# Adapter + mixture-of-experts + quantized FFN on one core: collecting in three segments of four, two and two blocks, five routing groups, three tile output buffers, and a new hand-off order

## The reference, cut to what matters

```python
h  = x @ W.T + (x @ A[adapter].T) @ Bm[adapter].T * scale          # layer 1, condition
s  = sigmoid(h @ gate_w.T); top_scores, sel = top_k(s, 2)          # routing, 2 of 8 experts
for k in range(2):
    xs = h * top_scores[:, k]
    routed += w2[sel] @ (silu(w1[sel] @ xs) * (w3[sel] @ xs))
x1 = x + routed + ws2 @ (silu(ws1 @ h) * (ws3 @ h))
y  = einsum('bct,bcd->bdt', x1, w[cond])                           # layer 2, condition
u  = relu(quant(fwht(y)) @ ternary(w_up).T) ** 2
x2 = x1 + quant(fwht(u)) @ ternary(w_down).T
```

## Time and profile before

| what | value |
|---|---|
| median of 3 runs | 372.76 us (369.45 to 373.54) |
| the profiled execution | 371.4 us |
| its span in the trace | 369.3 us |
| outside of the span | 2.1 us |
| mean granted TensorE clock | 0.97 of full speed |

### The profile page before, as it was taken

How to read it: one execution, slowest core, us unless ns; L and a number is a source line. 1 busy time by engine, 2 the same in 40 slices (tenths; PEclk the granted TensorE clock), 3 DMA queues, 4 the chain that set the end, 5 groups by cost and what they waited for, 6 DMA issues and landing times. The chain is left out here.

```text
span 369.3 us, 8740 instructions
## 1 busy us (share of the span) xinstructions
PE 318.8 (86%) x2564; PEld 296.8 (80%) x2564; DVE 278.4 (75%) x735; ACT 217.7 (59%) x528; POOL 204.0 (55%) x211
## 2 busy tenths in 40 slices
PE   7899999995757999949998989799987798887974
PEld 7798999894657999938997979799976687776863
DVE  0957999999587998743654557678956999997995
ACT  4574343232215467606566658788866888956964
POOL 1100059899899898930000667888818888883000
PEclk9999999999689999987999999999999999998999
DMA  7980692522237859547398885997757556664013
GB/s 187 359 330 1 228 313 84 198 74 76 88 104 209 261 192 303 191 114 215 109 286 265 190 171 89 197 211 141 173 145 137 70 75 107 123 101 79 30 58 114
DMA packets 53803, 59.02 MB, mean 160 GB/s; under 512 B 9856, under 2 KB 47744, under 8 KB 53760
## 3 DMA queue, kind: packets, MB, share of 16 engines
q1 hardware_dynamic: 40752, 40.81, 36.1%
q0 software_dynamic: 12432, 17.57, 23.4%
q10 hardware_dynamic: 576, 0.10, 0.2%
HBM read 32.87 MB, written 25.59 MB: 158 GB/s over the span
## 5 line engine op out<-in xcount | busy, mean ns | idle before, releaser
L1378 POOL DMA_INDIRECT X<-ys,POSY x64 | 101.9, 1592 | 74.7 <-DMA ys<-YS 43.0
L1026 POOL DMA_INDIRECT hs<-ZF,POS x64 | 64.3, 1005 | 10.6 <-issue 10.1
L1025 POOL MEMSET PACE<- 128x512 f32 x64 | 34.8, 543 | 33.7 <-DVE POS L1014 33.7
L1278 PE MATMUL UP<-WH,XSH 128*128 x142 | 42.9, 302 | 0.4 <-issue 0.2
L1278 PE MATMUL UP<-WH,XSL 128*128 x142 | 39.9, 281 | 0.0
L1278 PE MATMUL UP<-WL,XSH 128*128 x142 | 39.8, 280 | 0.0
L792 PE MATMUL AUX<-WH,ZR 128*128 128x264 f32 x128 | 26.0, 297 | 10.3 <-ACT ZF L815 10.1
L1258 ACT ACTIVATE XSH<-TR 128x512 fp32r<-128x512 f32 (+1 forms) x36 | 21.4, 594 | 22.2 <-PE TR L1245 20.0
L815 ACT ACTIVATE ZF<-AUX 128x264 f32<-128x264 f32 x32 | 12.0, 387 | 36.6 <-PE AUX L802 16.4
L1263 DVE TENSOR_TENSOR XSL<-TR,XSH 128x512 fp32r<-128x512 f32 (+1 forms) x36 | 24.4, 678 | 10.3 <-ACT XSH L1258 7.3
L792 PEld LDWEIGHTS AUX<-WH,ZR 128*128 128x128 f32 x128 | 21.3, 198 | 11.9 <-issue 11.2
(11 more groups left out here) (262 smaller groups left out, 997.0 us busy)
## 6 DMA issues: line engine op xcount, KB each, us to landing
ys<-YS SPq DMA_DIRECT2D x42, 256.0 KB
XIN<-hs SPq DMA_DIRECT2D x71, 132.0 KB
X<-in_x SPq DMA_DIRECT2D x8, 512.0 KB, 8.0
out<-X SPq DMA_DIRECT2D x16, 256.0 KB, 2.2
X<-in_WE SPq DMA_DIRECT2D x8, 384.0 KB, 7.9
ZF<-in_xT SPq DMA_DIRECT2D x4, 512.0 KB
XR<-in_xT SPq DMA_DIRECT2D x4, 512.0 KB
hs<-ZERO SPq DMA_DIRECT2D x8, 132.0 KB
```

What stands on the lines that cost most here:

```text
L1025: e.memset(PACE[:, :], 0.0).then_inc(S["pac"], 1)
L1026: e.indirect_dma_start(hs, bass.IndirectOffsetOnAxis(ap=POS[:, k, t0 + t:t0 + t + 1], axis=0), HT[:, slot + t, :], None).then_inc(s_st[b % ...
L1278: mm = e.matmul(UP[s % 2][:, c * 256:c * 256 + 256], v[:, r % 2, k, c * P:(c + 1) * P], w[:, cols], start=(n == 0), stop=(n == 5))
L1378: e.indirect_dma_start(X1[:, tt, :], None, ys[p], bass.IndirectOffsetOnAxis(ap=POSY[:, k, tt:tt + 1], axis=0), compute_op=ALU.add).then_in ...
```

## The change

- `SEGMENTS` (4, 8) becomes (4, 6, 8): blocks 0 to 3, 4 and 5, 6 and 7 are collected from three ys tensors. `CARRIED` follows: 7, 15, 23. The second segment waits for pairs 0 to 27, the third for all 36. Pairs 13 to 19 are stored three times and pairs 20 to 27 twice. `count`, `jumps` and `home` run three times.
- `GROUP_SIZES` (2, 2, 2, 2) becomes (1, 1, 2, 2, 2): five routing chains.
- YS gets a third buffer (`NY = 3`), and `y_out` waits for the store of three pairs before.
- `TIME` is new throughout, so the order on each engine is new; the places that matter are shown below.

```diff
-GROUP_SIZES = (2, 2, 2, 2)
-SEGMENTS = (4, 8)
+GROUP_SIZES = (1, 1, 2, 2, 2)
+SEGMENTS = (4, 6, 8)
...
+PIECES = max(2, PARTS)
+BIGGEST = max(_b - _a for _a, _b in zip((0,) + SEGMENTS, SEGMENTS))
...
-    "home": [103.4764, 149.4409],
+    "home": [105.6110, 129.0289, 158.4598],
...
+NY = 3
...
-              for i, n in enumerate((TILES[0] + 2 * CARRIED[0], TILES[1]))]
+              for i, n in enumerate([TILES[0] + 2 * CARRIED[0]] + [2 * c for c in CARRIED[1:-1]] + [TILES[1]])]
...
-        YS = sb("YS", [P, 2, 2, D])
+        YS = sb("YS", [P, NY, 2, D])
...
-                pieces = ((ORIGIN, LINE[:, PARTS, 0:NE], 0), (START[:, 0, :], LINE[:, 0, 0:NE], P * TILES[0]),
-                          (START[:, 1, :], LINE[:, 1, 0:NE], 0))
-                if p:
-                    pieces = ((START[:, 0, :], LINE[:, 0, 0:NE], 0), pieces[2])
-                else:
-                    pieces = pieces[0:2]
+                pieces = [(START[:, c, :], LINE[:, c, 0:NE], P * TILES[0] if p == 0 else 0) for c in range(p + 1)]
+                if p == 0:
+                    pieces = [(ORIGIN, LINE[:, PARTS, 0:NE], 0)] + pieces
...
-            return [(1, 2 * i)] + ([(0, TILES[0] + 2 * i)] if i < CARRIED[0] else [])
+            return [(k, (0 if k else TILES[0]) + 2 * i) for k in reversed(range(PARTS)) if i < CARRIED[k]]
...
-            put = 16 * sum(len(homes(q)) for q in range(r % 2, r - 1, 2))
+            put = 16 * sum(len(homes(q)) for q in range(r % NY, r, NY))
...
-                if r >= 2:
-                    e.wait_ge(s_y[r % 2], put)
+                if r >= NY:
+                    e.wait_ge(s_y[r % NY], put)
```

More of the change, by code:

```diff
@@ L57 @@
 TIME = {
-    "home": [103.4764, 149.4409],
[L59 to L85, removed]
+    "home": [105.6110, 129.0289, 158.4598],
+    "last_tables": [150.8858],
+    "jumps": [100.6280, 111.3651, 144.8223],
+    "count": [79.3267, 98.0063, 136.3136],
@@ new lines @@
+    "make_mask": [8.7495],
+    "load_later": [15.9370],
+    "make_origin": [15.1470],
+    "weight_sums": [44.7497],
+    "weight_total": [47.9447],
+    "ternary": [50.3145],
+    "clear_bd": [112.1478],
+    "load_x": [2.3500, 3.2900, 13.3920, 20.9885, 39.3378, 39.8078, 105.4953, 154.5733],
+    "x_hi": [8.5090, 9.5650, 23.5675, 34.8153, 48.1582, 65.2068, 78.9802, 90.7745],
+    "x_lo": [9.6185, 10.7610, 24.8810, 36.6353, 57.1475, 67.6288, 82.8875, 92.2764],
+    "xa": [11.2710, 14.0190, 29.7990, 40.9592, 58.4400, 69.3503, 84.1800, 94.5724],
@@ L104 @@
+        116.7551, 137.4616, 142.0748, 169.6800, 172.4670],
     "s_out": [
[L105 to L113 removed]
@@ L114 @@
-    "fold_hi": [23.6227],
-    "fold_lo": [23.9137],
+        24.2775, 37.8862, 49.1080, 67.0253, 77.0912, 81.9485, 84.4739, 88.6438, 96.4583, 103.6855, 116.0016,
+        120.0114, 140.6218, 143.2733, 170.5995, 173.6655],
+    "load_xT": [2.8200, 14.9970, 15.4670, 40.2778, 40.7478, 58.4400, 68.9213],
+    "fold_turn": [7.0760],
+    "fold_copy": [7.7350],
+    "fold": [12.6750],
+    "fold_shared": [8.6790],
+    "shared_hi": [12.8970],
+    "shared_lo": [15.2270],
+    "fold_hi": [14.2390],
+    "fold_lo": [14.9800],
@@ L462, in adapter_moe_quant_ffn @@
         s_st = [sem(f"p_st{i}") for i in range(RING)]
-        s_y = [sem(f"p_y{i}") for i in range(2)]
+        s_y = [sem(f"p_y{i}") for i in range(NY)]
         s_g = [[sem(f"p_g{k}{i}") for i in range(4)] for k in range(2)]
@@ L1349, in y_put @@
                 for k, slot in homes(r):
-                    e.dma_start(ys[k][slot * P:slot * P + n, :].rearrange("(c q) d -> q c d", q=P), YS[:, r % 2, 0:tiles, :])\
-                     .then_inc(s_y[r % 2], 16)
+                    e.dma_start(ys[k][slot * P:slot * P + n, :].rearrange("(c q) d -> q c d", q=P), YS[:, r % NY, 0:tiles, :])\
+                     .then_inc(s_y[r % NY], 16)
             at("sync", "y_put", r + 2, y_put)
         def puts_done(e, pairs):
-            for j in range(2):
-                e.wait_ge(s_y[j], 16 * sum(len(homes(q)) for q in range(j, pairs, 2)))
+            for j in range(NY):
+                e.wait_ge(s_y[j], 16 * sum(len(homes(q)) for q in range(j, pairs, NY)))
         def plan_collect(p):
```

122 lines of the change are left out of this document (64 added, 58 removed), and 248 rows, old and new, of the table TIME.

## The result

The changed kernel takes 377.17 us (median, 374.32 to 378.48) against 372.73 for the kernel before on the same chip: ratio 1.011 (95% interval 1.007 to 1.016), slower by a little over 1%. The forecast was 365 with a range up to 374. The profiled execution took 378.48 us (span 376.7) at a mean granted clock of 0.958; that of before took 371.4 (span 369.3) at 0.97. The one is the slowest of its four runs and the other lies under its median, so the spans differ by 7.4 us and the medians by 4.4. The spans of one kernel differ from run to run (the kernel before: mostly 367 to 373 us), so a difference of one to three us between two traces can be chance.

What follows compares the result with a forecast made beforehand. It took GpSimd's scatters, then its collects, as two chains in a row, VectorE close behind. Span 369.3 - 7 = 362.3, with 2.1 outside it 364.4, plus half of 1.4 for the profiled execution: 365, range 353 to 374.

Steps and rivals of the forecast that it cites:

- The first scatter: Start of GpSimd's scatters: needs block 0 alone, so it comes at 40.5 us in place of 49.8.
- The scatters: GpSimd starts 9 us earlier, then starves by as much for VectorE's positions; last scatter at about 161, term +1 (-6 to +6).
- From the last scatter to the first collect: Pairs 13 to 19 with added stores on SyncE's queue: +1 us (-2 to +5), first collect at 205.
- the slower case: Rival: VectorE and the queue make scatters and first stores late; last positions 141.7, loads up to 5 us later; 376, chance 0.12.
- VectorE's added steps at 0: Third home (4.9 us) and last_tables' four more instructions (0.9) lie beside the scatters' end: cost 0, at most 5.8.
- The collects: GpSimd's 64 collects: border stop's 7.4 us go, and 3 of 5.1 us of landing waits; end at 328, 8.5 earlier.
- Does the end follow?: Stretch up to the last finish: VectorE's idle falls, so the end moves 7 us for the collects' 8.5.
- VectorE holds the end: Third rival, at the end: collects end early but blocks wait for VectorE; only 1 to 3 us come, 367 to 371, chance 0.20.
- the early one: Rival: the early start carries through, VectorE's idle falls to 6 us, scatters end at 155; 358 to 359, chance 0.24.

Runs made afterwards that it cites:

- e1: The changed kernel with 14 memsets (7.7 us) on GpSimd ahead of the 32nd collect, where the border wait stood: 376.82 us.
- e8: The changed kernel with the first add-subtract step of layer 2 cut to 32 of 256 columns in the ten blocks behind the pairs: 371.36 us.
- e12: The changed kernel without the fifth routing group, GROUP_SIZES (2, 2, 2, 2): 383.26 us.
- e15: The changed kernel with the 15 added stores cut to 32 of 256 columns, the rest filled with zeros near 80 us: 368.68 us.
- e4: The kernel before with 15 more stores, of pairs 13 to 27, to a tensor nobody reads: 376.56 us.
- e10: All parts of the change (three segments, five groups, three buffers) in the order of the kernel before: 376.84 us.
- e11: e10 without the third segment, so five groups and three buffers in the old order: 368.94 us.
- e13: e10 with last_tables put right behind the last jumps, ahead of the added home: 381.25 us.
- e14: e10 with the 15 added stores cut to 32 of 256 columns, the rest filled with zeros near 80 us: 376.59 us.
- e2: The changed kernel and its order with two segments (4, 8) again, 15 stores less: 378.76 us.
- e3: The kernel before, in its own order with its four groups and two buffers, with three segments (4, 6, 8): 377.66 us.
- e5: The kernel before with the same 15 extra stores as e4, issued by ScalarE instead of SyncE: 377.29 us.
- e6: The kernel before with three buffers of YS in place of two, nothing else: 371.38 us.
- e7: The kernel before with five routing groups (1, 1, 2, 2, 2) in its own order: 371.41 us.
- e9: The kernel before with the 15 extra stores of e4 on SyncE, each row cut from 256 columns to 32: 374.02 us.

## Why the prediction was wrong, step by step

**The first scatter** was right: 40.5 forecast, 41.4 measured. **The scatters:** stops of 8 to 10 us in sum forecast, 10.9 measured, released by the cast as foreseen; last scatter at 161 forecast, 162.55 measured (160.99 and 160.23 in e1 and e8). The mechanism, VectorE taking the chain over, held. The sentence that the early start is lost there needs a limit: e12 shows that in this order it would have been 6 us worse without the fifth group.

**From the last scatter to the first collect** was mis-sized: +1 forecast (-2 to +5), 3.8 measured; with the bytes cut (e15) the idle time is 44.39 in place of 46.71. The step counted only the one store ahead of pair 19's last as surely in the way, 0.9 us. e4 shows 4.8 us for seven extra stores in this stretch, close to the 6 us of DMA time that the same paragraph had worked out and then set aside as hidden in the free 0.30. A mean share of 0.70 was no cover. With the first collect at 209.26 the prediction's own sign of the slower case (over 209) was met, though its condition, last positions later than 139, was not: the last group's scatters start at 135.62.

**VectorE's added steps at 0** was too low as well. last_tables did end behind the last scatter (its cast starts at 163.44 in the changed kernel, at 150.09 before), but it is phase 1's last pairs, and SyncE's loads behind their stores, that come late (e10, e11, e13). What the third segment costs ahead of the first collect beside its bytes is about 2 us: 46.6 in e14 against 44.2 in e11, 44.4 in e15 against 42.6 in e2, 50.1 in e3 against 47.7 in e4.

**The collects** were right: 123.2 forecast, 123.5 measured, no stop left. That more stores "may cost some back" beside them had no price in the sum; the pairs took 3.3 us longer there. Most of that is the new order and not the stores: e2 has the order without the added stores and takes 71.55 us against 69.31, and e4 has the stores without the order and takes 68.82.

**"Does the end follow?" is the step that failed.** It let the end move 7 us for the collects' 8.5, arguing that VectorE's idle time would fall from 21.8 to 11.3 us, since that around the border had its cause taken away. It was 20.6 (under 13 was the sign to look for), with 8.0 around the border where 7.0 had been. From the collects' end to the end of the span the prediction had 362.3 - 328 = 34 us, and 44.0 were measured. The end hung on the last pair from the start. Before, the border's collect waited for that pair's store, so the collects' end was itself the last pair plus a constant: 96.2 to 96.95 us from the last `y_out` to the end in the kernel before and in e4, e5, e6, e7, e9 and e11. Taking the stop away gives only what the way over layer 2's own work is shorter than that: 94.7 to 94.9 in the changed kernel, e3, e10 and e14, so about 2 us. The constant is rough: in the new order e1, e12 and e15 have 89.6 to 92.8. e1 shows the rest of the collects' gain as slack, and e8 that VectorE's work is on that way. Against these 2 us stand the added stores, which make the last pair itself late. The third rival, "VectorE holds the end" (chance 0.20), had the mechanism; it gave 367 to 371 because it too took the pairs to be on time. The price on the pairs is from the slower rival, which put it down to the loads' place in the queue; by e5 the queue is not what costs, as far as that run can tell.

The sum as measured, on the span: +2.5 scatters, +3.8 to the first collect, +3.3 beside the collects, -2.1 tail = +7.4 (on the medians +4.4). The largest single cause is when the bytes are written: with them moved, the changed kernel is 8.5 us faster (e15), and in the kernel before the stores alone cost 3.6 (e4), of which an eighth of the bytes gives back half (e9). The trace of e15 accounts for 5.5 of it in the stretches behind the last scatter. In the old order the third segment as a whole costs 7.9 (e10, e11), and how much of that is bytes is open, since e14's median gives nothing back.

One sum of the prediction is off beside this: the parts that its range is said to leave out (the far half of the slower case, a small part of the early one) come to about 0.1 by its own chances, not to nearly 0.2.

## What to carry to other kernels

Before pricing a stop on one engine, look at what ends it: if the producer it waits for also feeds the end by another way, only the difference of the two ways is to be had, and a pause put in the stop's place shows in one run whether the engine's gain is slack. Copies that buy an earlier start are paid where the producers wait for their stores, and that need not be where the DMA engines are fullest: seven stores at a mean share of 0.73 cost 4.8 us, eight at 0.91 beside the collects nothing (e4). So ask in which stretch they are written and who waits there, before counting a mean busy share as room. And when a change is made of parts, time them apart: groups and buffers alone were worth 1%, hidden under the segment's loss.

## What was not expected of the hardware

- From the last scatter to the first collect, where the mean DMA share was 0.69 and rose to 0.73, seven stores of 256 KB made the first collect 4.8 us late (e4); eight more of them from there to the last pair, where it was 0.81 and rose to 0.91, added nothing (68.8 us in place of 69.4). Issued from ScalarE all fifteen delayed the last pair by 7.2 us in the profiled execution (e5), from SyncE by 4.3. Seven eighths of the bytes written near 80 us, where 71.8:102.6 had 89 GB/s and a share of 0.26 and then had 201 and 0.60, cost nothing that can be seen (e15).
- In front of the first block of layer 2 whose `mix` products stand in UP, TensorE stood for 4.09 us in the changed kernel, because ScalarE waited for stores of finished blocks (timeline):

```profile
290.14 0.38 ACT L1467 ACTIVATE X<-UP 128x256 f32<-128x256 f32 x1 [3.47 <-DMA out<-X]
...
290.55 0.75 DVE L1471 TENSOR_TENSOR X<-UP,X 128x256 f32<-128x256 f32 x2 [3.71 <-ACT X L1467]
...
291.45 0.77 PE L1484 MATMUL UP<-CON,X 128*128 128x128 f32 x2 [4.09 <-DVE X L1471]
```

ScalarE's wait was 2.2 us in the kernel before, and 2.1 (e1), 1.1 (e12), 1.9 (e15) and 4.0 (e8) in other kernels of the new order. So it is not the fuller pairs' stretch that makes it long, since e1 has that too; its cause is open.
